# A graph layer in fp32: the order of sums, placings and the two dense layers within one step, and the place of the dst and weight loads

## What is computed

```python
x, src, dst, edge_attr_48            # (12500, 128), (412500,), (412500,), (412500, 48)
agg = segment_sum(edge_attr_48, dst, 12500)
h = maximum(layernorm(x), 0)
x_in = concatenate([h, agg, broadcast(graph_globals[0])], axis=1)    # 128 + 48 + 64
out = x + relu(x_in @ W1 + b1) @ W2 + b2                             # hidden 256
```

## Time and profile before

| | before |
|---|---|
| median of 3 executions | 277.83 us |
| the profiled execution | 278.3 us |
| its span, first to last instruction | 276.5 us |
| PE busy | 243.8 us (88%) |
| DVE busy | 239.1 us (86%) |
| ACT busy | 147.3 us (53%) |
| POOL busy | 75.5 us (27%) |
| bytes moved | 94.53 MB, mean 342 GB/s |

### The profile page before, as it was taken

One profiled execution on the slowest core, in us unless ns is written; L12 is line 12 of the kernel. 1 busy time (PEld: TensorE's weight loads), 2 busy tenths in 40 slices (PEclk: granted clock), 3 DMA queues, 4 the chain that ended last, 5 costly groups with the idle time before them and its releaser, 6 DMA issues.

```text
span 276.5 us, 17261 instructions
## 1 busy us (share of the span) xinstructions
PE 243.8 (88%) x7448; PEld 195.0 (71%) x7448; DVE 239.1 (86%) x579; ACT 147.3 (53%) x315; POOL 75.5 (27%) x89
## 2 busy tenths in 40 slices
PE   7445688998999999999999999999999988998893
PEld 5344676786697688778777877886787776777572
DVE  2993589999899999999999899899899899886394
ACT  3466285465365556555555655564465454557640
POOL 8470310412213303303312311321330330234210
PEclk9977599999999999999999999999999999999998
DMA  7999999999999999999999999999999999981101
GB/s 247 377 383 260 367 382 381 381 381 382 389 384 387 392 388 385 388 391 385 388 392 387 386 390 391 383 387 382 372 390 390 385 384 369 382 295 59 40 38 57
DMA packets 70876, 94.53 MB, mean 342 GB/s; under 512 B 4324, under 2 KB 64260, under 8 KB 70854
## 3 DMA queue, kind: packets, MB, share of 16 engines
q1 hardware_dynamic: 69802, 94.29, 95.3%
q10 hardware_dynamic: 956, 0.00, 0.2%
q0 software_dynamic: 96, 0.00, 0.0%
HBM read 87.88 MB, written 6.40 MB: 341 GB/s over the span
## 4 chain that ended last, share of the span: by engine, by line
DMA 63%; PE 14%; DVE 9%; issue 7%; SPq 3%; POOL 1%; ACT 1%; DVEq 0%; POOLq 0%
DMA out<-out_buf 56%; PE group_bank L1021 5%; DMA edge_buf<-in_edge_attr 3%; DMA x_buf<-in_x 3%; PE out_bank L1087 3%; SPq L326 2%; DVE onehot L776 2%; PE window_bank L1044 2%; DVE rel_rows L731 2%; PE hidden_bank L1004 1%; POOL out_buf L513 1%; PE hidden_bank L1069 1%; DVE tile_sums L839 1%; DVE bn L818 1%; PE out_bank L1059 1%
## 5 line engine op out<-in xcount | busy, mean ns | idle before, releaser
L776 DVE TENSOR_TENSOR onehot<-rel,const_bank 128x896 f32<-128x896 f32 (+1 forms) x122 | 122.8, 1026 | 7.4 <-PE group_bank L1021 7.2
L1021 PEld LDWEIGHTS group_bank<-edge_buf,onehot 128*32 128x32 f32 x6454 | 78.8, 112 | 21.3 <-issue 15.9
L1021 PE MATMUL group_bank<-edge_buf,onehot 128*32 128x48 f32 x6454 | 86.1, 210 | 8.8 <-issue 6.1
L513 POOL TENSOR_TENSOR out_buf<-mlp_out,xb_buf 128x512 f32<-128x512 f32 x23 | 29.5, 1283 | 163.5 <-DMA out<-out_buf 137.3
L1069 PE MATMUL hidden_bank<-normed_t,w_node 128*128 128x512 f32 (+1 forms) x100 | 50.5, 586 | 0.1
L1087 PE MATMUL out_bank<-w_sb,hidden 128*128 128x128 f32 x384 | 47.7, 277 | 1.4 <-ACT normed_t L587 1.4
L1087 PEld LDWEIGHTS out_bank<-w_sb,hidden 128*128 128x128 f32 x384 | 44.7, 192 | 1.6 <-issue 1.6
L576 ACT ACTIVATE normed_x<-x_buf,shift,inverse 128x128 f32<-128x128 f32 x98 | 40.4, 482 | 5.9 <-DVE shift L833 5.9
L1073 PE MATMUL hidden_bank<-tile_sums,w_high 112*128 112x512 f32 (+1 forms) x50 | 38.7, 775 | 0.0
L501 POOL TENSOR_TENSOR xb_buf<-x_buf,b_rows 128x512 f32<-128x512 f32 (+1 forms) x25 | 31.9, 1277 | 22.8 <-DMA x_buf<-in_x 10.5
L608 ACT ACTIVATE hidden<-hidden_bank,hidden_bias 128x512 f32<-128x512 f32 (+1 forms) x50 | 31.8, 668 | 4.7 <-PE hidden_bank L1075 4.6
(11 more groups left out here) (92 smaller groups left out, 217.0 us busy)
## 6 DMA issues: line engine op xcount, KB each, us to landing
edge_buf<-in_edge_attr SPq DMA_DIRECT2D x97, 672.0 KB, 10.4
edge_buf<-in_edge_attr SPq DMA_DIRECT2D x24, 504.0 KB, 10.2
x_buf<-in_x SPq DMA_DIRECT2D x24, 256.0 KB, 8.9
out<-out_buf SPq DMA_DIRECT2D x23, 256.0 KB, 9.4
dst_rows<-in_dst SPq DMA_DIRECT2D x3, 448.5 KB, 10.6
dst_rows<-in_dst SPq DMA_DIRECT2D x1, 252.3 KB
out<-out_buf SPq DMA_DIRECT2D x1, 224.0 KB
edge_buf<-in_edge_attr SPq DMA_DIRECT2D x1, 168.0 KB, 9.1
```

The source lines that it names most:

```text
L513: pool.tensor_tensor(out_buf[k.parity][:, 0:nj, :], mlp_out[:, 0:nj, :], xb_buf[k.third][:, 0:nj, :], ALU.add).then_inc(out_added, 1)
L776: dve.tensor_tensor(onehot[:, c0:c0 + cols, :], rel[:, r0:r0 + cols].unsqueeze(2).to_broadcast([P, cols, WINDOW]), ramp_const.unsqueeze(1) ...
L1021: done = pe.matmul(group_bank[h][WINDOW * j:WINDOW * (j + 1), n * F_EDGE:(n + 1) * F_EDGE], onehot[:, (g0 + j) * EDGES_PER_ROW + r, :], ed ...
```

## The change

On PE, a step now sums both parts in one run, then transposes a tile, runs the first layer, places both parts, and runs the second layer. Before, the sums of part 0 were followed by the placing of the step before's part 1, the transposes and the first layer, and the sums of part 1 by the placing of part 0 and the second layer. One `pe.If` guards a step's work in place of several, and the work stands in the code three times.

On DVE, the adds, placings and statistics follow the five one-hots and `invert` in one run, both adds one behind the other. The statistics of tile s + 1 stand at the end of step s; before, they stood in step s + 1.

On ACT, both copies of sums stand together and `tile_high` comes one step earlier in the text. The last tile is turned into `group_bank[1]`.

SP loads blocks 1 to 3 of `dst` at the ends of steps 0 to 2, the weights of both layers in step 0, and b2 and what the bias needs behind the edges of step 1. The blocks are turned in PE's steps 3, 5 and 7, with one buffer `rel_rows` in place of two, and the masks of the repeated edges are written in step 10 in place of step 4.

```diff
             load_dst(0)
             load_part(At(0), 0)
             load_part(At(0), 1)
-            load_dst(1)
             load_x(At(0))
             load_part(At(1), 0)
-            load_dst(2)
-            load_dst(3)
-            load_weights()
             load_part(At(1), 1)
+            load_bias()
             load_x(At(1))
             for s in range(steps):
...
                     load_part(At(s + 2), 0)
+                if s == 0:
+                    load_weights()
                 if s >= 4:
                     store(At(s - 4))
                 if s + 2 < steps:
                     load_part(At(s + 2), 1)
+                if 1 <= s + 1 < blocks:
+                    load_dst(s + 1)
```

ACT's program:

```diff
             for s in range(2, full_steps):
-                tile_high(At(s - 2))
                 if s >= 3:
                     copy_out(At(s - 3))
+                if s % 2 == 0 and 2 <= s // 2 <= blocks:
+                    copy_rel(s // 2 - 1)
                 copy_sums(At(s), 0)
+                if s == 2:
+                    split_weights()
+                copy_sums(At(s), 1)
                 copy_turned(At(s - 1))
                 deviate(At(s))
                 relu_hidden(At(s - 2))
-                copy_sums(At(s), 1)
                 normalise(At(s))
+                tile_high(At(s - 1))
+                if s % 2 == 0 and s // 2 < blocks:
+                    relative(s // 2)
+                if s == 2 * blocks + 2:
+                    load_ends(1)
```

DVE's program, ahead of the loop and in it:

```diff
             low_sums(At(0), 0)
+            low_sums(At(0), 1)
             moments(At(0))
             join_moments(At(0))
-            invert(At(0))
             for q in PART_QUADS[1]:
                 make_onehot(At(1), q)
+            invert(At(0))
+            moments(At(1))
+            join_moments(At(1))
+            make_onehot(At(2), 0)
+            make_onehot(At(2), 1)
             dve.wait_ge(agg_zeroed, 4)
-            dve.sem_inc(agg_added, 3)
-            dve.sem_inc(tile_low_ready, 2)
+            add_window(At(0), 0)
+            add_window(At(0), 1)
+            make_placing(At(1), 0)
+            make_placing(At(1), 1)
+            low_sums(At(1), 0)
+            low_sums(At(1), 1)
+            for q in (2, 3, 4):
+                make_onehot(At(2), q)
             for s in range(1, full_steps):
                 n = At(s + 1)
-                add_window(At(s - 1), 0)
-                low_sums(At(s - 1), 1)
-                if n.value * GROUPS % P + GROUPS > P:
-                    dve.wait_ge(rel_ready, 2 * (n.value * GROUPS // P + 2))
-                make_onehot(n, 0)
                 if s >= 2:
+                    if n.value * GROUPS % P + GROUPS > P:
+                        dve.wait_ge(rel_ready, 2 * (n.value * GROUPS // P + 2))
+                    make_onehot(n, 0)
+                    if s == 2:
+                        dve.wait_ge(w1_high_ready, 1)
+                        dve.tensor_tensor(w1_low[:, :], w1_edge[:, :], w1_high[:, :].bitcast(fp32), ALU.subtract)\
+                           .then_inc(w1_split, 1)
                     tile_low(At(s - 2))
-                moments(At(s))
-                make_onehot(n, 1)
-                join_moments(At(s))
-                make_placing(At(s), 0)
-                make_onehot(n, 2)
-                add_window(At(s - 1), 1)
-                low_sums(At(s), 0)
...
+                    make_onehot(n, 1)
+                    low_sums(At(s), 0)
+                    make_onehot(n, 2)
+                    low_sums(At(s), 1)
+                    make_onehot(n, 3)
+                    make_onehot(n, 4)
                 invert(At(s))
-                make_onehot(n, 3)
-                make_onehot(n, 4)
-                make_placing(At(s), 1)
-                if s == blocks:
+                add_window(At(s), 0)
+                add_window(At(s), 1)
+                make_placing(n, 0)
+                if s + 1 < full_steps:
+                    make_placing(n, 1)
+                k = last_tile() if s + 1 == tiles - 1 else n
+                moments(k)
+                join_moments(k)
+                if s == 2 * blocks + 2:
...
             second, last = At(tiles - 2), last_tile()
-            add_window(At(full_steps - 1), 0)
-            low_sums(At(full_steps - 1), 1)
-            moments(last)
-            make_placing(At(steps - 1), 0)
+            invert(last)
             tile_low(At(tiles - 3))
-            join_moments(last)
-            invert(last)
-            add_window(At(full_steps - 1), 1)
             low_sums(At(steps - 1), 0)
             add_window(At(steps - 1), 0)
```

PE's program:

```diff
+            def layers_and_places(s):
+                turn_x(s.plus(-1))
+                first_layer(s.plus(-2))
+                place(s, 0)
+                place(s, 1)
+                second_layer(s.plus(-2))
+
             with pe.Fori(0, full_steps // 2) as i:
                 even, odd = At(0, i), At(1, i)
                 sum_part(even, 0)
-                with pe.If(i > 0):
-                    place(even.plus(-1), 1)
-                    turn_x(even.plus(-1))
-                    first_layer(even.plus(-2))
                 sum_part(even, 1)
                 with pe.If(i > 0):
-                    place(even, 0)
-                    second_layer(even.plus(-2))
-                with pe.If(i < 1):
+                    pe.wait_ge(rel_ready, i * 2)
+                    layers_and_places(even)
+                with pe.Else():
                     turn_places()
-                    turn_rel(1)
                 sum_part(odd, 0)
...
                 sum_part(odd, 1)
...
+                with pe.If(i >= blocks):
+                    layers_and_places(odd)
+                with pe.Else():
+                    with pe.If(i > 0):
+                        layers_and_places(odd)
+                        turn_rel(i)
+                    with pe.Else():
+                        place(At(0), 0)
+                        place(At(0), 1)
+                        turn_x(At(0))
+                        sum_bias()
+                        place(At(1), 0)
+                        place(At(1), 1)
+
+            third, second, last = At(tiles - 3), At(tiles - 2), last_tile()
             turn_x(second)
-            sum_part(final, 0)
+            sum_part(At(steps - 1), 0)
             first_layer(third)
-            place(final, 0)
-            turn_x(last)
+            place(At(steps - 1), 0)
+            turn_x(last, group_bank[1])
```

More of the change, by code:

```diff
@@ L539, in relative @@
                 act.wait_ge(neg_first_ready, b)
-                act.activation(rel_rows[0:rows, b % 2, :], dst_rows[0:rows, b, 0:group_edges], ACT.Identity,
+                act.activation(rel_rows[0:rows, :], dst_rows[0:rows, b, 0:group_edges], ACT.Identity,
                                bias=neg_first[0:rows, b:b + 1]).then_inc(rel_rows_ready, 1)
@@ L550, in copy_rel @@
                                    .rearrange("p (r g) -> p r g", g=P)[:, :, 0:rows], ACT.Copy)\
-                        .then_inc(rel_ready, 1)
+                        .then_inc(rel_ready, 2 * steps if (b, h) == (blocks - 1, 1) else 1)
             def copy_sums(s, h):
@@ L578, in normalise, with copy_turned @@
                 done.then_inc(normed, 1)
-            def copy_turned(k):
+            def copy_turned(k, from_bank=turned_bank):
                 act.wait_ge(x_turned, k.value + 1)
@@ L586, in copy_turned @@
                 cols = strips_of(k) * P
-                act.activation(normed_t[k.parity][:, 0:cols], turned_bank[:, 0:cols], ACT.Copy)\
+                act.activation(normed_t[k.parity][:, 0:cols], from_bank[:, 0:cols], ACT.Copy)\
                    .then_inc(turned_copied, 1)
@@ L654, in _ @@
             copy_sums(At(0), 0)
-            relative(1)
             zero_strip(3)
             copy_sums(At(0), 1)
-            copy_rel(1)
-            relative(2)
             deviate(At(0))
             normalise(At(0))
-            load_ends(1)
+            deviate(At(1))
             copy_sums(At(1), 0)
-            copy_rel(2)
-            relative(3)
+            copy_sums(At(1), 1)
             copy_turned(At(0))
-            split_weights()
-            copy_rel(3)
-            deviate(At(1))
             bias()
-            copy_sums(At(1), 1)
             normalise(At(1))
+            tile_high(At(0))
             for s in range(2, full_steps):
-                tile_high(At(s - 2))
                 if s >= 3:
                     copy_out(At(s - 3))
+                if s % 2 == 0 and 2 <= s // 2 <= blocks:
+                    copy_rel(s // 2 - 1)
                 copy_sums(At(s), 0)
+                if s == 2:
+                    split_weights()
+                copy_sums(At(s), 1)
                 copy_turned(At(s - 1))
@@ L680, in _ @@
                 relu_hidden(At(s - 2))
-                copy_sums(At(s), 1)
                 normalise(At(s))
-            second, last = At(tiles - 2), last_tile()
-            tile_high(At(tiles - 3))
+                tile_high(At(s - 1))
```

(26 more changed lines are left out.)

69 lines of the change are left out of this document (25 added, 44 removed).

## The result

The changed kernel takes 299.2 us (median of 4 runs, 298.9 to 299.3) against 277.7 us (276.9 to 278.1) beside it: 1.078 times the time before, 95% interval 1.075 to 1.080. The span grows from 276.5 to 297.2 us. The forecast had the sign and the main mechanism, and gave a quarter of the size: +5.5 us where it is +21.5.

The account below looks back on a forecast made before the run. Transfers led narrowly, with PE and DVE near full; after the change DVE bounds. Span 276.5 + 8.0 (steps) + 0.4 (w1_low) - 0.8 (head) - 2.1 (tail) = 282.0; + 1.8 - 0.5 = 283.3 us, range 278.3 to 287.5.

Parts of the forecast that it names:

- DVE's work of 8.95 us: DVE's step before the change: 9.74 us less 0.23 waiting for PE and 0.56 behind the shift.
- Term (1): DVE's step: the first add's register load, uncovered behind the shift, costs 0.73 us a step (bounds 0 and 0.73).
- Term (2): DVE's step: the second add, directly behind the first with its own register load, costs 0.37 us more (bounds 0 and 0.37).
- Term (3): DVE's step: join_moments waits for the last of its own statistics, 0.89 us in place of 0.79, so 0.10.
- DVE's step of 10.11: DVE's step after the change, added up by instruction, against 9.73 before: DVE becomes the bound, +8.0 us over 21 steps.
- case C: Rival: shift or tile_low meets GpSimd on the shared port in all 21 steps, 0.5 us each: 293 us; chance 0.05.
- Head, -0.8: Start of the kernel: onehot of step 3 at 40.5 us in place of 41.33; bounds -3.5 and +2.
- Tail, -2.1: From the onehot of step 24 to its add: 13.2 us in place of 15.25; the rest, DVE alone, unchanged.
- Loads, no effect: Reordered loads: up to 2.0 us of the DMA stream, none reaching the end with DVE as the bound.
- A: Rival: the transfers lead, DVE's step 9.0 us as its sequencer runs ahead: 277.0 to 279.0, likeliest 278.7; chance 0.16.
- B: Rival: faster, the stream gains 2.0 us and PE's shorter path holds: 274.9 us of span; chance 0.08.
- D: Rival: the loop's code leaves PE's instruction memory, +9 us a step, near 470 us; chance 0.02.

Follow-up runs that it names:

- the experiment: The changed kernel with POOL's x_plus_b2 made to wait until tile_low of that step has run: 291.7 us, 7.5 less than the changed kernel.

## Why the prediction was right or wrong

**What bounds the kernel before, and DVE's work of 8.95 us: right.** With one load uncovered the step's floor is 9.61, the sum of that work and 0.65 us of idle time. One reading beside it is off: of SyncE's 44 waits for PE half are longer than "a microsecond at most", the longest 2.3; nothing rests on it.

**Term (1), the uncovered load, 0.73 us: right.** Shift and add are 0.81 us from start to start; moving the load gives 0.63 to 0.64, since the add still can't start closer than 0.18 behind the shift.

**Term (2), the second add, 0.37 us: right in size, for the most part wrong in cause.** Taking its load away gives 0.10 to 0.11. The rest of the gap is the wait for the first add, which comes with putting the two side by side and not with the load.

**Term (3), 0.10: right;** the first join starts 0.9 us behind the statistics in each step.

**DVE's step of 10.11: right where POOL is out of the way** (10.15 there), **and too short by 0.4 us in the kernel as it is.** The step of the prediction that failed is case C: a meeting of `tile_low` with POOL in each step was given 0.05, and the sum holds nothing for it. In the changed kernel 21 of 25 calls are held. In the kernel before it was 4, and 8 shifts, one of them the 0.71 us of the earlier trace rows; POOL mostly waited for the stores (137.3 us, 19 times). With DVE as the bound it waits for ACT's copy instead, in all 23 calls (186.6 us), so `x_plus_b2` comes at a fixed place: from 153 to 270 us `tile_low` lasts 1.07 to 1.09 us in 11 of 12 calls. Case C priced a meeting at 0.5 us; here it is 0.4. The meetings cost 7.6 us by the held time and 7.5 by the experiment. The rule of the Trainium skill (SBUF — State Buffer, SBUF: two separate sides) that case C cites holds here: 0.69 us becomes 1.08 under `x_plus_b2`, and 1.51 under `add_out`, and both times `tile_low` ends 0.54 to 0.55 us behind POOL's operation (207.13 and 206.58; 187.14 and 186.60), as it does in every call of these two traces that is held by 0.1 us or more.

**The steps together.** 21 x (10.11 - 9.73) = 8.0 and 0.4 for `w1_low` forecast, 7.2 for the `tile_low` held in these steps (0.4 more lies in the tail), and 1.9 left over: 17.5 measured. With the hold taken away steps average 10.23, 0.08 over the unheld 10.15, most of it in the first ones and a few of 10.4 to 10.5 later; that part wasn't taken apart.

**Head, -0.8: wrong by 5.9 us.** The failing step is the time given to the end of step 1's sums, 28 to 31 us. They ended at 35.3, and the first add, put at about 31, started at 36.67: 5.7 of the 5.9. The count of stops, four in place of three, was right up to the first placing; but the last of the four ended only at 34.75, and a fifth of 2.6 us followed. The prediction doesn't show how it came from the stops to its 28 to 31 us, so what in it was mis-sized stays open. DVE's work from the add to the statistics of tile 2 was put at 8.2 us and took 8.6. The upper bound of +2 stands without a working, and a first placing one piece of code later, with all of DVE's queue behind it, lay outside it.

The Trainium skill (Runtime: NRT & Kernel Launch, Instruction fetch mechanics) calls the cost of crossing into the next 16 KiB block "mostly hidden". These runs differ: in the first pass PE stopped 3.0, 3.2, 4.0 and 2.6 us for its code, each time in the middle of a run of like matmuls. The DMA engines were full of edges meanwhile; that this made the stops long wasn't tested.

**Tail, -2.1: right;** it is -1.9, with DVE alone at the end as said.

```profile
281.57 0.51 DVE L806 TENSOR_TENSOR agg<-agg,window_bank 48x352 f32 x1 [2.04 <-PE window_bank L1055]
...
292.32 0.69 DVE L851 TENSOR_TENSOR out_buf<-out_bank,xb_buf 128x512 f32<-128x512 f32 x1
```

**Loads, no effect: right** within 1 us. The DMA rate fell further than the 375 GB/s named as a sign, to 359, as the step is longer than forecast.

**The rivals.** A is what the kernel becomes once both loads are hidden and POOL is clear: 277.0 to 279.0 forecast for it, 278.9 and 279.0 measured. Its working also holds, the statistics of tile 23 at 247.2 and 248.1 against 247.67; only DVE's step is 9.41 there and not 9.0. B needs the transfers to end earlier, which they didn't. D is ruled out: PE's queue fetched 8 pieces of code in the run, five of them in the loop's first pass and only one in the loop after it, at 66.0 us.

```profile
q8 instruction: 8, 0.13, 0.2%
```

**The sum.** 283.3 + 7.2 (POOL) + 1.9 (rest of the steps) + 5.9 (head) + 0.2 (tail) = 298.5, against 299.2; the median lies 2.0 us over the profiled span, where 1.3 were taken. The range ended at 287.5, where its two upper margins of 2.9 and 2.8 add up to 289.0; neither figure has room for the held `tile_low` or for a first placing 5 us later, and both follow from the new order.

## What to carry to other kernels

Where DVE sets the step, a register load from SBUF cost 0.63 us when it stood behind an instruction at which the sequencer itself waits, and where the transfers set it 2.7 us in the whole run; put it ahead of that instruction, beside long operations. When an order makes another engine the bound, look again at who now triggers each engine that shares a port with it: work that used to drift past gets a fixed place, and a meeting then costs in every step. If two repairs of one stretch each give next to nothing (0.6 and 0.3 us here, 3.3 together), try them together before either is dropped.

## What had not been expected of the hardware

The sequencer of DVE runs ahead of the engine past queued operations, but in these traces not past the shift, which waits for the reciprocal. In the kernel before, the load for an add at 147.32 ran from 144.61, right behind the start of the shift and under two onehots and a placing. In the changed kernel it ran at 211.53, again right behind the start of the shift (211.51), and the add had to wait for it.

An operation of DVE that POOL holds doesn't slow down in proportion; in these traces it ends a fixed time behind POOL's, 0.55 us for `tile_low` and 0.02 us for the shift (in the earlier trace rows 256.60 against 256.58). So the same meeting costs from 0.1 to 1.1 us, by how much of POOL's 1.27 us is left when DVE's operation starts.
